# Setup of a four-layer MoE block rebuilt: one load of small arrays, loads in order of need, batch 0's weight first, other setup behind batch 0's and 2's gating

## The reference, cut to what matters

```
# layer 0, cond: a LoRA mixture, weights w = cond_8[b]
out = x @ W_base.T + b_base + 2.0 * sum_e w[b,e] * (x @ As[e].T) @ Bs[e].T
# layer 0, ffn
n1 = layernorm(out); rw = gating(n1, smha_sim, smha_gates)      # 8 experts
q, k, v = (sum_e rw[..., e] * n1 @ W[e] for W in (q_proj, k_proj, v_proj))
hs = out + sum_e rw[..., e] * softmax(causal(q @ k.T)) @ v @ o_proj[e]
n2 = layernorm(hs); rw2 = gating(n2, moe_sim, moe_gates)
x = x + hs + sum_e rw2[..., e] * gelu(n2 @ w1[e]) @ w2[e]
gating(h, sim, gates): logits = normalize(h) @ normalize(sim) - sigmoid(gates); relu; softmax over the active experts
# layer 1, cond: the expert argmax(cond_8[b]) as a gated MLP; ffn: a MoE
# layer 2, cond: softmax of cond_8[b], the two best of 8 experts and their weights
```

## Time and profile before

| | |
|---|---|
| three timed runs | 1203.39, 1207.82, 1209.09 us, median 1207.82 |
| profiled execution | 1204.67 us, of which 1202.8 us span |
| PE busy | 86% of the span (weight loads 64%) |
| DVE, ACT, POOL busy | 64%, 43%, 13% |
| mean granted TensorE clock | 0.937 of full |

### The profile page before, as it was taken

The page is one execution under the profiler, slowest core; times in us unless marked ns, Lnnn a source line. Parts: engine busy times, 40 slices in busy tenths (PEclk is TensorE's granted clock), DMA queues, the critical chain, the costliest instruction groups (busy, mean ns, idle before and its releaser), DMA issues.

```text
span 1202.8 us, 18237 instructions
## 1 busy us (share of the span) xinstructions
PE 1033.0 (86%) x6758; PEld 765.6 (64%) x6758; DVE 765.6 (64%) x1828; ACT 518.1 (43%) x836; POOL 158.3 (13%) x166
## 2 busy tenths in 40 slices
PE   1799999998657899999999964878999999998855
PEld 1688988887445667767767633556666666666432
DVE  3365556655384578888888886447477675676542
ACT  1235443525341354664467322234545545453420
POOL 0121111100125500000000004201112012021000
PEclk8699999999677999999999986989999999999986
DMA  9000000000020130011300003000000000000000
GB/s 313 30 1 15 15 14 15 1 15 14 26 98 1 53 123 30 25 53 53 123 1 1 1 1 107 1 1 1 2 5 1 6 1 5 6 1 5 5 5 5
DMA packets 13097, 35.40 MB, mean 29 GB/s; under 512 B 3738, under 2 KB 7370, under 8 KB 12240
## 3 DMA queue, kind: packets, MB, share of 16 engines
q1 hardware_dynamic: 12624, 33.01, 7.9%
q10 hardware_dynamic: 288, 1.18, 0.2%
q0 software_dynamic: 96, 0.04, 0.0%
HBM read 33.16 MB, written 1.06 MB: 28 GB/s over the span
## 4 chain that ended last, share of the span: by engine, by line
PE 59%; issue 18%; DVE 15%; DVEq 4%; ACT 2%; POOL 1%; POOLq 1%; ACTq 0%
PE ps L1105 5%; PE ps L826 5%; PE ps L1093 5%; PE ps L990 4%; PE ps L1035 3%; PE ps L1245 3%; PE ps L1166 3%; PE ps L1146 2%; PE ps L1010 2%; DVE arena L1801 2%; PE ps L1184 2%; PE ps L860 2%; PE ps L836 2%; PE ps L872 2%; PE ps L883 2%
## 5 line engine op out<-in xcount | busy, mean ns | idle before, releaser
L1903 DVE TENSOR_REDUCE arena<-ps 128x8 f32<-128x2048 f32 x32 | 73.3, 2291 | 37.4 <-PE ps L1146 37.4
L1450 ACT ACTIVATE arena<-ps 128x2048 f32<-128x2048 f32 x32 | 60.1, 1878 | 57.9 <-PE ps L1170 57.9
L1093 PE MATMUL ps<-uR,arena 128*128 128x256 f32 x256 | 74.6, 386 | 0.0
L1035 PE MATMUL ps<-arena 128*128 128x128 f32 x512 | 66.8, 286 | 6.1 <-DVE arena L1817 4.8
L1010 PE MATMUL ps<-arena,uR 128*128 128x512 f32 x128 | 68.7, 619 | 3.4 <-ACT arena L1396 3.0
L1035 PEld LDWEIGHTS ps<-arena 128*128 128x128 f32 x512 | 64.2, 200 | 11.2 <-issue 7.3
L1105 PE MATMUL ps<-arena 128*128 128x256 f32 x256 | 63.9, 395 | 6.7 <-DVE arena L1884 3.7
L1245 PE MATMUL ps<-arena 128*128 128x512 f32 x128 | 64.6, 627 | 5.5 <-DVE xacc L1977 4.4
L1423 ACT ACTIVATE arena<-ps 128x512 f32<-128x512 f32 x64 | 38.0, 598 | 60.5 <-PE ps L1094 54.1
L1105 PEld LDWEIGHTS ps<-arena 128*128 128x128 f32 x256 | 47.8, 194 | 20.0 <-issue 9.6
L826 PE MATMUL ps<-arena 128*128 128x256 f32 x256 | 58.8, 388 | 0.0
(11 more groups left out here) (377 smaller groups left out, 2350.5 us busy)
## 6 DMA issues: line engine op xcount, KB each, us to landing
arena<-in_skills SPq DMA_DIRECT2D x16, 768.0 KB, 5.7
arena<-in_expert_w SPq DMA_DIRECT2D x2, 2048.0 KB, 8.0
arena<-in_l_experts SPq DMA_DIRECT2D x8, 386.5 KB, 3.2
arena<-in_consts_b ACTq DMA_DIRECT2D x1, 1152.0 KB, 7.6
...
```

The source lines that it names most:

```text
L1035: last = mm(high[:, 2, t * P:(t + 1) * P], eD[h][:, k, col:col + P], uT[u][:, k, :], start=k == 0, stop=k == 1)
L1093: mm(o, phiC[:, st_ * P:(st_ + 1) * P], uR[:, b, :], start=True, stop=False)
L1450: av(pexp[:, t, gp].rearrange("p c h t -> p (c h t)"), scores[:, :, :].rearrange("p c t -> p (c t)"), ACT.Exp, scale=SCALE3).then_inc(s.sc ...
L1903: V.tensor_reduce(nm[:, k, :, 2 * gp:2 * gp + 2], scores[:, :, :].rearrange("p c (h t) -> p c h t", h=2), X, ALU.max, negate=True).then_in ...
```

## The change

- The 12 small arrays are laid side by side in one array `head` (128 x 588 words) and loaded by one DMA. The constants are loaded in three pieces: `ident` and `ones` (with `head` on `setup_loaded`), `causal` and `selR` (`spread_loaded`, with `cond` and `condc`), and the rest (with `b_loads`). SP issues them in order of need; x is now issued by ACT, and `consts_b` by SP, behind q and k.
- DVE's setup is: scale batch 0's `bsw`, square `sims`, `gsig`, `weff` of batch 0, normalise `sims`. PE's is one 128-column matmul for batch 0 and the sum of squares.
- The rest is put into the lists as steps. WB (DVE): `bsw` of batches 1 to 7. WM (PE): their product. WF (DVE): their `weff`. RCA, RX, RCB (DVE, ACT, DVE): the routing. CV (ACT): the conversion to bf16.
- The gates have a buffer of their own, and POOL clears it without a wait; before it was `bsw`'s. `consts_b` is staged where `S8m` will be. Waits for the split loads stand where their data are read first.

```diff
@@ SP
-            for dst, src in setup_loads:
-                sp.dma_start(dst, src).then_inc(s.setup_loaded, 16)
-            sp.dma_start(x2R[:, 0, :], A["x"][0]).then_inc(s.inputs0, 16)
-            for b in range(1, NB):
-                sp.dma_start(x2R[:, b, :], A["x"][b]).then_inc(s.inputs1, 16)
-            for dst, src in w0_loads:
+            sp.dma_start(head, A["head"]).then_inc(s.setup_loaded, 16)
+            sp.dma_start(cst[:, 0:FIRST], A["consts_f"][:, 0:FIRST]).then_inc(s.setup_loaded, 16)
+            for dst, src in w0_loads[:2]:
+                sp.dma_start(dst, A[src]).then_inc(s.qk_loaded, 16)
+            for dst in (cond, condc):
+                sp.dma_start(dst[:, :, :], A["cond_bc"]).then_inc(s.spread_loaded, 16)
+            sp.dma_start(cst[:, FIRST:SPREAD], A["consts_f"][:, FIRST:SPREAD]).then_inc(s.spread_loaded, 16)
+            sp.dma_start(cbf_f32, A["consts_b"]).then_inc(s.consts_loaded, 16)
+            sp.dma_start(cpart[:, :], A["consts_p"]).then_inc(s.consts_loaded, 16)
+            for dst, src in w0_loads[2:]:
                 sp.dma_start(dst, A[src]).then_inc(s.w0_loaded, 16)
+            sp.dma_start(cst[:, SPREAD:], A["consts_f"][:, SPREAD:]).then_inc(s.b_loaded, 16)
@@ PE
-            pe.wait_ge(s.setup_loaded, all_setup)
+            pe.wait_ge(s.setup_loaded, 32)
             pe.wait_ge(s.setup_ready, 1)
-            for h in range(2):
-                last = mm(PF[0][:, h * 512:(h + 1) * 512], ascat,
-                          bsw[:, 4 * h:4 * h + 4, :].rearrange("p b o -> p (b o)"), start=True, stop=True)
-            last.then_inc(s.setup_mm, 1)
+            mm(PF[0][:, 0:P], ascat, bsw[:, 0, :], start=True, stop=True).then_inc(s.setup_mm, 1)
...
-            pe.wait_ge(s.sim_ready, 1)
-            pe.wait_ge(s.consts_bf, 1)
...
+                if n == "WM":
+                    pe.wait_ge(s.setup_ready, 3)
+                    for lo, hi in ((1, 4), (4, 8)):
+                        last = mm(PF[0][:, lo * P:hi * P], ascat, bsw[:, lo:hi, :].rearrange("p b o -> p (b o)"), start=True, stop=True)
+                    last.then_inc(s.setup_mm, 1)
...
+                        if g == 0 and b == 0:
+                            pe.wait_ge(s.spread_loaded, 16 * 3)
+                            pe.wait_ge(s.weff_ready, 3)
@@ ACT
-            act.dma_start(cbf_f32, A["consts_b"]).then_inc(s.consts_loaded, 16)
-            act.dma_start(cpart[:, :], A["consts_p"]).then_inc(s.consts_loaded, 16)
-            act.wait_ge(s.consts_loaded, 32)
-            av(cbf[:, :], cbf_f32, ACT.Copy)
-            act.wait_ge(s.setup_loaded, 16 * len(setup_loads))
-            av(identb[:, :], ident, ACT.Copy).then_inc(s.consts_bf, 1)
+            act.dma_start(x2R[:, 0, :], A["x"][0]).then_inc(s.inputs0, 16)
+            for b in range(1, NB):
+                act.dma_start(x2R[:, b, :], A["x"][b]).then_inc(s.inputs1, 16)
+            act.wait_ge(s.setup_loaded, 32)
             for g in range(2):
                 last = av(gsig[g], gsig[g], ACT.Exp, scale=-1.0)
             last.then_inc(s.sig_exp, 1)
-            act.wait_ge(s.cond_diff, 1)
-            av(cond[:, :, :], cond[:, :, :], ACT.Exp)
-            av(wsel[:, :, :], wsel[:, :, :], ACT.Exp).then_inc(s.sig_exp, 1)
-            act.drain()
@@ DVE
+            V.tensor_scalar(bsw[:, 0, :], bscat, w16[:, 0:1], 2.0, ALU.mult, ALU.mult).then_inc(s.setup_ready, 1)
...
+            V.tensor_tensor(weff[:, 0, :], PF[0][:, 0:P], wbaseT, ALU.add).then_inc(s.weff_ready, 1)
...
+                if n == "WB":
+                    for j in range(1, NB):
+                        last = V.tensor_scalar(bsw[:, j, :], bscat, w16[:, j:j + 1], 2.0, ALU.mult, ALU.mult)
+                    last.then_inc(s.setup_ready, 1)
+                if n == "WF":
+                    dve.wait_ge(s.setup_mm, 3)
+                    V.tensor_tensor(weff[:, 1:NB, :], PF[0][:, P:NB * P].rearrange("p (b o) -> p b o", b=NB - 1),
+                                    wbaseT.unsqueeze(1).to_broadcast([P, NB - 1, P]), ALU.add).then_inc(s.weff_ready, 1)
+                if n == "RCA":
+                    dve.wait_ge(s.spread_loaded, 48)
...
+                if n == "RCB":
+                    dve.wait_ge(s.sig_exp, 2)
@@ ORDER_A, the first line of PE's list
-    COND.0 NT0.0 LOG0.0 GTR0.0 COND.1 SPR0.0 NT0.1 QK.0 LOG0.1 SC.0 VT.0 PT.0 GTR0.1 AT.0 SPR0.1 COND.2 O1.0
+    COND.0 NT0.0 LOG0.0 WM.0 GTR0.0 COND.1 SPR0.0 NT0.1 QK.0 LOG0.1 SC.0 VT.0 PT.0 GTR0.1 AT.0 SPR0.1 COND.2 O1.0
```

More of the change, by code:

```diff
@@ L125 @@
     "ACT": """
-    AF0.0 GX0.0 GTR0.0 RW0.0 RW1.0 AF0.1 QKC.0 EX.0 GX0.1 VC.0 PTC.0 GTR0.1 RW0.1 RW1.1 QKC.1 VC.1 AF1.0 AF0.2
+    AF0.0 GX0.0 GTR0.0 RW0.0 RW1.0 AF0.1 QKC.0 CV.0 EX.0 GX0.1 VC.0 PTC.0 GTR0.1 RW0.1 RW1.1 QKC.1 VC.1 AF1.0 AF0.2 RX.0
     EX.1 PTC.1 GX1.0 GU0.0 GU1.0 GTR1.0 GX0.2 GTR0.2 AF1.1 SI0.0 RW0.2 RW1.2 SI1.0 GU0.1 AF0.3 GX1.1 GU1.1 DN.0
@@ L134 @@
     "DVE": """
-    LN0.0 NH0.0 GA0.0 GB0.0 GE0.0 LN0.1 S8A0.0 NH0.1 S8A1.0 GA0.1 MXA.0 GB0.1 GE0.1 S8B0.0 S8B1.0 S8A0.1 LN0.2
-    S8A1.1 NH0.2 LN1.0 NH1.0 MXA.1 GA1.0 GB1.0 GA0.2 GE1.0 S8B0.1 GB0.2 S8B1.1 S8M0.0 GE0.2 S8M1.0 LN1.1 NH1.1
+    WB.0 LN0.0 NH0.0 GA0.0 GB0.0 GE0.0 WF.0 LN0.1 S8A0.0 NH0.1 S8A1.0 GA0.1 MXA.0 GB0.1 GE0.1 S8B0.0 S8B1.0 S8A0.1 LN0.2
+    S8A1.1 RCA.0 NH0.2 LN1.0 NH1.0 MXA.1 GA1.0 RCB.0 GB1.0 GA0.2 GE1.0 S8B0.1 GB0.2 S8B1.1 S8M0.0 GE0.2 S8M1.0 LN1.1 NH1.1
     X1.0 LN0.3 HM0.0 GA1.1 S8A0.2 NH0.3 S8A1.2 HM1.0 GB1.1 GE1.1 GA0.3 LA.0 GB0.3 MXA.2 S8M0.1 GE0.3 S8M1.1 L1.0
@@ L503, in build, with in_head @@
         w0 = {n: ta([P, E, P]) for n in ("q", "k", "v", "o", "w1", "w2")}
-        ascat, bscat, wbaseT = ta([P, P]), ta([P, P]), ta([P, P])
-        bbase = ta([P, P])
-        w16 = ta([P, NB])
+        head = ta([P, HEADW])
+        head_at = [0]
+        def in_head(n):
+            head_at[0] += n
+            return head[:, head_at[0] - n:head_at[0]]
+        ascat, bscat, wbaseT, bbase = (in_head(P) for _ in range(4))
+        w16, lnp = in_head(NB), in_head(4)
+        sims = [in_head(E) for _ in range(2)]
+        gsig = [in_head(E) for _ in range(2)]
+        wg1, bg1 = in_head(16), in_head(16)
+        assert head_at[0] == HEADW
         bsw = ta([P, NB, P])
         weff = ta([P, NB, P])
-        lnp = ta([P, 4])
-        sims = [ta([P, E]) for _ in range(2)]
         simsq = ta([P, 2, E])
         simn, simt = ta([P, 2 * E]), ta([P, 2 * E])
-        gsig = [ta([P, E]) for _ in range(2)]
-        wg1, bg1 = ta([P, 16]), ta([P, 16])
         EXPW = 3 * T + 5
@@ L523, in build @@
         nrm, nsq = [nC, x1C], [sqC, y1C]
-        gate_words = bsw.rearrange("p b o -> p (b o)")
-        gate4 = [[bsw[:, 4 * g + 2 * u:4 * g + 2 * u + 2, :].rearrange("p k (c r) -> p k c r", c=4) for u in range(U)]
+        gate_words = ta([P, NB * P])
+        gate4 = [[gate_words[:, (2 * g + u) * T:(2 * g + u + 1) * T].rearrange("p (k c r) -> p k c r", k=K, c=4) for u in range(U)]
                  for g in range(2)]
@@ L534, in build @@
         S8a = [ta([P, E, T]) for _ in range(U)]
-        S8m = [ta([P, E, T]) for _ in range(U)]
+        both8m = ta([P, U * E * T])
+        S8m = [both8m[:, u * E * T:(u + 1) * E * T].rearrange("p (e t) -> p e t", e=E) for u in range(U)]
+        cbf_f32 = both8m[:, 0:NBF]
         qkC = [ta([P, 2, T]) for _ in range(U)]
@@ L665, in nth @@
             return sum(w.split(".")[0] in steps.split() for w in words[:words.index(word) + 1])
-        setup_loads = []
-        def arriving(dst, name):
-            setup_loads.append((dst, A[name]))
         w0_loads = [(w0[n], "L0_" + k) for n, k in (("q", "q_proj"), ("k", "k_proj"), ("v", "v_proj"), ("o", "o_proj"),
                                                     ("w1", "w1"), ("w2", "w2"))]
[L674 to L679, removed]
+        FIRST = CONSTS["causal"][0]
+        SPREAD = CONSTS["samep"][0]
         b_loads = [(l1w1, "l1w1"), (l1w2, "l1w2"), (l1b1, "l1b1"), (l1g, "l1g"), (shw, "shared"),
@@ L1318, in step_a @@
                            wide[:, 2 * h:2 * h + 2, :].rearrange("p c t -> p (c t)"), ACT.Gelu).then_inc(s.gelu_ready, 1)
+                if n == "RX":
+                    act.wait_ge(s.cond_diff, 1)
+                    av(cond[:, :, :], cond[:, :, :], ACT.Exp)
+                    av(wsel[:, :, :], wsel[:, :, :], ACT.Exp).then_inc(s.sig_exp, 1)
+                if n == "CV":
+                    act.wait_ge(s.consts_loaded, 32)
+                    av(cbf[:, 0:], cbf_f32[:, 0:], ACT.Copy)
+                    av(identb[:, :], ident, ACT.Copy).then_inc(s.consts_bf, 1)
                 if n == "QKC":
@@ L1510, in rsqrt @@
                 dr()
-            dve.wait_ge(s.setup_loaded, 16 * len(setup_loads))
-            for b in range(NB):
-                last = V.tensor_scalar(bsw[:, b, :], bscat, w16[:, b:b + 1], 2.0, ALU.mult, ALU.mult)
-            last.then_inc(s.setup_ready, 1)
+            dve.wait_ge(s.setup_loaded, 32)
```

(1 more changed line is left out.)

118 lines of the change are left out of this document (63 added, 55 removed).

## The result

The changed kernel takes 1194.65 us (median of 10 runs, 1192.7 to 1200.49), the kernel before 1203.55 in the same comparison (10 runs). The ratio is 0.9922, with a 95% interval from 0.9904 to 0.994: 0.8% faster, 0.6% to 1.0%. In a later comparison with more rounds on one chip the two medians were 1194.31 and 1207.55, a ratio of 0.9897 (0.9872 to 0.9922). The forecast was 1193.6 with a range of 1187 to 1202.

What follows compares the result with a forecast made beforehand. PE is busiest by far, so setup can only move the start of its dense stream. -13.4 (LN0.0) + 2.2 (RCB.0) - 3.0 (clock) = -14.2 from 1204.67 gives 1190.5, plus 3.15 to the median: 1193.6 us, range 1187 to 1202.

Steps and rivals of the forecast that it cites:

- The landing: Setup loads: `head`, `ident` and `ones` land at about 5.4 us, bounds 4.4 and 8.1.
- ACT: Setup on ACT: eight DMA issues end at 4.8, table load at 6.1, exps at 6.4 us; DVE waits for these.
- LN0.0: First layer norm of batch 0 on DVE: starts at 12.5 us instead of 25.86, -13.4 us.
- Hidden steps: Setup work moved into the later chain on PE, DVE and ACT, taken to cost 0 behind other engines' work.
- WM.0: PE, behind LOG0.0: 3.3 us of matmuls hidden by DVE's and ACT's gating; up to 3.3 without that cover.
- WF.0: DVE, behind GE0.0: 1.1 us, cost 0 because COND.1 waits for ACT's copy anyway; bound 1.1.
- CV.0: ACT, between QKC.0 and EX.0: conversion of `cbf`, cost taken as 0; bound 2.1 us.
- RCA.0: DVE, behind S8A1.1: at most 2.8 us, cost 0 beside QK.1 and VT.1; 2.8 without that cover.
- RCB.0: DVE, between GA1.0 and GB1.0: delays GTR1.0 while PE has no other work, +2.2 us; bounds 0 and 3.0.
- The clock: PE during batch 0's gating: WM.0's matmuls lift the granted clock, shortening SPR0.0 and QK.0, -3.0 us; otherwise 0.
- the clock stays low: Rival: PE's clock stays low until QK.0, so -11.2 us in sum, 1196.6 us; chance 0.35.
- the experts' load, the slower rival: Layer-1 experts' loads on SP wait for RCB.0; slower only if landing beyond 118 us, 1221 us at 125; chance 0.03.

Runs made afterwards that it cites:

- the second execution: The changed kernel profiled a second time without any edit: 1192.55 us, one run.
- the second pair: The kernel before and the changed kernel, each profiled a second time without any edit: 1207.04 and 1192.55 us, one run each.
- the order of work alone: Against the kernel before: the changed lists and steps, but the 15 loads in SP's old order on one semaphore, x behind them; 1200.34 us, ratio 0.9956.
- the loads alone: Against the kernel before: only the loads changed, the setup's work left where and in the order it was; 1208.03 us, ratio 1.0015.
- The third execution of the changed kernel: The changed kernel profiled a third time without any edit; span 1197.1 us.
- the profiled pair: The first profiled executions of the kernel before and the changed kernel: 1204.67 and 1194.49 us.

## Why the prediction was right, step by step

- **The landing (forecast 5.4; measured 4.96, 4.71 and 4.79 in three executions).** Right within the bounds. ACT's queue took less of the traffic than half: 0.29 of the 0.96 MB moved by 5.0 us. As forecast, it did not matter, since ACT's exps bind.
- **ACT (exps end at 6.4; measured 6.82, and 6.3 in the second execution).** The eight issues ended at 5.19 (forecast 4.8) and at 4.7. Taking the issues out of the way gained 1.0 to 1.5.
- **LN0.0 (12.5; 12.14, 11.60, 11.69).** The term was -13.4 and measured -13.7 (-14.2 in the second pair). `sims` took 3.3 (3.4), WB.0 1.46 (1.45). Of the 13.7, the order of work alone gave 8.0 and the loads alone 0.4; the rest needs both.
- **Hidden steps.** WM.0 and WF.0 as told above. CV.0 runs on ACT from 39.84 to 42.15, and EX.0 needs MXA.0, which is over at 42.20: 0. RCA.0 runs from 52.10 to 54.4, beside QK.1 (51.56 on): 0. A loss of 0.4 between NT0.0 and GTR0.0 (7.78 us apart, 7.37 before) was not forecast. It came with the moved work: the order alone has it too (7.78), the loads alone do not (7.43). Most of it is one place: DVE's memset in GB0.0 (L1638) starts 0.44 behind the operation ahead of it in place of 0.11, after 0.28 of idle for which the profile names no releaser, and only for batch 0. Why is open.
- **RCB.0 (+2.2; measured +2.1 by the rows, 2.0 by moving it).** Mechanism and size were right. Where it matters the step was not needed: it has a place in DVE's idle time, with the experts' load still early enough.
- **The clock (-3.0) is the term that was mis-sized.** From the start of GTR0.0 to the start of LOG0.1, with COND.1, SPR0.0 and QK.0 between them, it took 16.85 before and 16.05 now: -0.8. In the second pair it is -2.4 (17.19 and 14.76). The third execution of the changed kernel has 16.44: -0.4 against the first profile of the kernel before, -0.75 against the second. The failed step is the sentence that named L762 as the nearest row, "after them the clock was high until 21.1". The column did say 1.00 there, but L762's four passes of 512 columns took 3.75 us, and the same kernel has four passes of the same shape near its end that took half:

```profile
1191.17 1.99 PE L1245 MATMUL ps<-arena 128*128 128x512 f32 x4 [0.78 <-DVE xacc L1977]
```

L762 ran at 1.2 GHz, so it is no example of dense work at a high clock, and no row shows a high clock between it and 21.1. WM.0 ran at that level as well: 3.33 us for 1792 columns are 1.86 ns a column, L762's 1.83, where QK.1's 7.10 for 8192 are 0.87. The second step that failed is that a clock lifted by WM.0 would stay up for QK.0: PE has only sparse work from GTR0.0 to NT0.1, and in every execution NT0.1 or the start of QK.0 was slow again (no QK.0 took less than 8.35, where QK.1 takes 7.10).
- **The sum.** By the profiled pair -10.2, forecast -14.2. From 85 us on, I had taken the rest to be as long as before. In the profiled pair the lead does stay at 11.35 from 89 to 295 us; behind that it moves in steps between 10.5 and 13.5. I put these down to half-rate stretches, which fall at other places in each execution, but did not trace them one by one. Three executions of the changed kernel had spans of 1192.6, 1190.8 and 1197.1. The second pair differs by 14.4 at the end, the first by 10.2 (spans). By the medians it is -8.9 in its own comparison and -13.2 in the later one. That the median (1194.65) was met within 1.1 us is therefore partly luck: the clock term was too large by 0.6 to 2.6, the 0.4 was missing from the sum, and the kernel before came out 4.3 lower in that comparison than the 1207.82 from which I had started.

The rivals: "the clock stays low" (1196.6) describes the first execution best; the experts' load, the slower rival, was issued at 68.28, took 3.0 to 4.1 to land and so had 12 us to spare before UG0.0 (10 were forecast).
